# A Mamba mixer and cross-attention layer in fp32 on one core: the decay product in 64x64 tiles, its weights made by VectorE alone, keys loaded over 128 partitions

## What is computed

```python
h    = rmsnorm(x) * norm_w
gate, hid, B, C, dt = split(h @ in_proj.T)          # 8192, 8192, 8*128, 8*128, 128 wide
hid, B, C = silu(causal_conv(hid, B, C))            # 4 taps
dt   = softplus(dt + dt_bias);  A_cs = cumsum(-exp(A_log) * dt)
# 128 heads of 64, 8 groups of 16 heads; one chunk holds the whole sequence
M[i,j,h] = (C_i . B_j)[group of h] * exp(A_cs[i,h] - A_cs[j,h])   for j <= i, else 0
y[i,h]   = sum_j M[i,j,h] * hid[j,h] * dt[j,h] + Dp[h] * hid[i,h]
yg   = y * silu(gate);  yg = yg * rsqrt(mean over each group of yg**2) * gnorm_w
x    = layernorm(x + x + yg @ out_proj.T)
x    = layernorm(x + softmax(x @ ctx.T) @ ctx)       # per sequence
x    = layernorm(x + x @ W_base.T + b + 2 * (top-2 of 8 experts, rank 16))
```

## Time and profile before

| what | value |
|---|---|
| median of 3 runs | 1558.09 us (1551.89 to 1561.17) |
| profiled execution | 1558.3 us, span of its instructions 1556.6 us |
| busy share of the span | TensorE 95%, weight loads 77%, VectorE 69%, ScalarE 48%, GpSimd 43% |
| mean granted clock of TensorE | 0.978 of full |
| mixer, to about 1205 us of the span | TensorE all but always busy; transfers take 19 to 27% of the transfer engines |
| attention, from about 1250 us | transfer engines 98% busy at first, TensorE 79 to 85% |

### The profile page before, as it was taken

One profiled execution on the slowest core, in us unless ns is written; L12 is line 12 of the kernel. 1 busy time (PEld: TensorE's weight loads), 2 busy tenths in 40 slices (PEclk: granted clock), 3 DMA queues, 4 the chain that ended last, 5 costly groups with the idle time before them and its releaser, 6 DMA issues.

```text
span 1556.6 us, 25685 instructions
## 1 busy us (share of the span) xinstructions
PE 1471.4 (95%) x10492; PEld 1204.2 (77%) x10492; DVE 1071.3 (69%) x1248; ACT 754.2 (48%) x1003; POOL 661.6 (43%) x433
## 2 busy tenths in 40 slices
PE   5999999999999999999999999999999768889886
PEld 4888988898888889898989898989888534444442
DVE  5785878487757756774778477848784765767664
ACT  5764636462655355445546553646363254333330
POOL 6354537453645455454635554645373500001100
PEclk9999999999999999999999999999999879999998
DMA  4421212121312222121212121313120789888830
GB/s 149 122 80 57 87 51 92 55 83 49 92 52 69 62 79 68 52 82 58 82 38 93 55 83 48 93 45 88 50 82 7 181 187 211 191 183 206 188 72 12
DMA packets 53139, 141.52 MB, mean 91 GB/s; under 512 B 9684, under 2 KB 9812, under 8 KB 46858
## 3 DMA queue, kind: packets, MB, share of 16 engines
q1 hardware_dynamic: 51326, 136.20, 32.5%
q0 software_dynamic: 1696, 3.67, 1.0%
HBM read 135.72 MB, written 2.29 MB: 89 GB/s over the span
## 4 chain that ended last, share of the span: by engine, by line
PE 78%; issue 10%; DVE 6%; DMA 3%; ACT 2%; POOL 1%; SPq 0%; ACTq 0%; POOLq 0%; DVEq 0%
PE bank L1126 42%; PE bank L1193 20%; PE bank L1169 6%; PE bank L1156 3%; DMA x1p<-acc 2%; PE bank L1348 2%; PE bank L1321 1%; DVE conv L796 1%; DVE decay L849 1%; PE bank L1297 1%; DVE keysT L900 1%; PE bank L1180 0%; PE bank L1317 0%; DVE wo_lo L826 0%; DVE part L757 0%
## 5 line engine op out<-in xcount | busy, mean ns | idle before, releaser
L1126 PE MATMUL bank<-h_hi,w_hi 128*128 128x448 f32 x1152 | 337.5, 374 | 2.3 <-DVE conv L796 2.3
L1126 PE MATMUL bank<-h_lo,w_hi 128*128 128x448 f32 x1152 | 327.2, 365 | 0.0
L1126 PE MATMUL bank<-h_hi,w_lo 128*128 128x448 f32 x1152 | 326.6, 365 | 0.0
L796 DVE SCALAR_TENSOR_TENSOR conv<-bank,conv_w,conv 128x880 f32<-128x880 f32 (+2 forms) x240 | 268.1, 1117 | 79.4 <-ACT conv L571 73.7
L410 POOL TENSOR_TENSOR y_lo<-yg,y_hi 128x896 fp32r<-128x896 f32 x64 | 135.8, 2121 | 348.1 <-DVE mixw L859 202.2
L1126 PEld LDWEIGHTS bank<-h_hi,w_lo 128*128 128x128 f32 x1152 | 216.4, 188 | 17.3
L1126 PEld LDWEIGHTS bank<-h_lo,w_hi 128*128 128x128 f32 x1152 | 216.4, 188 | 17.0
L1126 PEld LDWEIGHTS bank<-h_hi,w_hi 128*128 128x128 f32 x1152 | 207.9, 188 | 24.2 <-DVE conv L796 3.2
L394 POOL TENSOR_TENSOR w_lo<-w_raw,w_hi 128x512 fp32r<-128x512 f32 x144 | 194.9, 1356 | 72.6 <-issue 36.4
L426 POOL TENSOR_TENSOR mixw<-decay,cbm 64x896 f32<-64x896 f32 x64 | 154.7, 2418 | 163.9 <-ACT decay L631 92.5
L837 DVE TENSOR_TENSOR hd_dt<-bank,dt_j 128x512 f32<-128x512 f32 x128 | 82.4, 686 | 177.7 <-PE bank L1156 177.5
(11 more groups left out here) (163 smaller groups left out, 2137.2 us busy)
## 6 DMA issues: line engine op xcount, KB each, us to landing
w_raw<-in_w_in SPq DMA_DIRECT2D x144, 256.0 KB, 2.9
decay<-cs_scratch SPq DMA_DIRECT2D x128, 196.0 KB
ring_a<-in_context SPq DMA_DIRECT2D x12, 1792.0 KB
ring_b<-in_context SPq DMA_DIRECT2D x12, 1792.0 KB
wo_raw<-in_w_out SPq DMA_DIRECT2D x64, 256.0 KB, 2.6
ring_a<-in_context SPq DMA_DIRECT2D x12, 208.0 KB
ring_b<-in_context SPq DMA_DIRECT2D x12, 208.0 KB
acc<-in_x SPq DMA_DIRECT2D x1, 1792.0 KB, 8.2
```

Source lines behind the costliest of these rows:

```text
L796: v.scalar_tensor_tensor(out=dst[:, :, sh:LEN], in0=src[:, :, 0:LEN - sh], scalar=conv_w[:, bass.ds(col, 1), TAPS - 1 - sh], in1=dst[:, :, ...
L1126: last = mm(place, w[:, k * P:(k + 1) * P], x[:, k, half * HALF:(half + 1) * HALF], start=(k == 0 and i == 0), stop=(k == KT - 1 and i == 2))
```

## The change

Four edits. First, `y_product` takes each sequence by itself: 64 rows by 64 channels stationary, 64 rows by 56 columns moving, so four small matmuls for a pair and not two: two row halves by two column halves of the array. The two sequences of a pair write to different banks of `yt` (even sequences bank 4, odd ones bank 5). `mixw` has no zero quarters and is half as wide, and every later buffer moves by that much. Second, VectorE makes the whole of `mixw` in one instruction over 128 partitions (`weigh`); GpSimd's `mix_low` and `after_mix_high`, and the zero fill, are gone, and one semaphore `m_done` stands for the two. Third, since even and odd sequences lie in two banks, `add_skip` is two instructions over 8 sequences each. Fourth, `load_unit` takes each sequence by itself, 128 partitions from a flat view of the rows (the last three rows belong to the next sequence and aren't used); the last sequence alone is cut in 112 and 13. VectorE also waits for its own `p_done` before the first `keys_part`.

```diff
-        mixw = sb("mixw", [P, 2, PAIRS, 2 * LEN], f32, mix)
+        mixw = sb("mixw", [P, 2, PAIRS, LEN], f32, mix)
...
+        def every_other(ap, b):
+            return ap.rearrange("p (q b) i -> p b q i", b=2)[:, b]
...
-            eng.wait_ge(unit_loaded[slot_of(unit)], 32 * (unit // RING + 1) + 16)
+            eng.wait_ge(unit_loaded[slot_of(unit)], 32 * (unit // RING + 1) + 16 * (unit // KR == PAIRS - 1))
...
# SP, load_cs
-                wait(sp, s["m_lo_done"], CT, g, c - 3)
-                wait(sp, s["m_hi_done"], CT, g, c - 3)
+                wait(sp, s["m_done"], CT, g, c - 3)
...
# SP, load_unit
-                src = A["context"][2 * u:2 * u + 2, :, r * UNIT:(r + 1) * UNIT]
-                for lo, hi in ((0, 112), (112, KP)):
-                    sp.dma_start(piece(unit)[lo:hi], src[:, lo:hi, :].rearrange("q p n -> p q n")
-                                 ).then_inc(unit_loaded[slot_of(unit)], 16)
-                if unit < RING:
-                    sp.dma_start(piece(unit)[KP:P], src[:, 0:P - KP, :].rearrange("q p n -> p q n")
-                                 ).then_inc(unit_loaded[slot_of(unit)], 16)
+                for q in range(2):
+                    first = (2 * (unit // KR) + q) * KP
+                    spans = ((0, P),) if first + P <= SEQS * KP else ((0, 112), (112, KP))
+                    for lo, hi in spans:
+                        sp.dma_start(piece(unit)[lo:hi, q, :],
+                                     rows[first + lo:first + hi, r * UNIT:(r + 1) * UNIT]
+                                     ).then_inc(unit_loaded[slot], 16)
...
# GpSimd
-            g_.memset(mixw[:].rearrange("p a b n -> p (a b n)"), 0.0)
...
-                    mix_low(g, st - 1)
-                    after_mix_high(g, st - 1)
...
# VectorE, add_skip
-                v.scalar_tensor_tensor(out=seqs(yg[:, c % 2, :]), in0=real(hid[:, c % 2, :]),
-                                       scalar=skip[:, bass.ds(g * CT + c, 1)], in1=bank_seqs(yt),
-                                       op0=ALU.mult, op1=ALU.add).then_inc(s["yres_done"], 1)
+                for b in range(2):
+                    last = v.scalar_tensor_tensor(out=every_other(seqs(yg[:, c % 2, :]), b),
+                                                  in0=every_other(real(hid[:, c % 2, :]), b),
+                                                  scalar=skip[:, bass.ds(g * CT + c, 1)],
+                                                  in1=yt[:, b, :].rearrange("p (q i) -> p q i", i=PAD)[:, :, 0:LEN],
+                                                  op0=ALU.mult, op1=ALU.add)
+                last.then_inc(s["yres_done"], 1)
...
# VectorE, mix_high becomes weigh
-                    out=mixw[PAD:P, :, :, LEN:2 * LEN],
-                    in0=decay[PAD:P, c % 4, :].rearrange("p (h q i) -> p h q i", h=2, i=LEN), scalar=1.0,
-                    in1=bc(cbm[PAD:P, :, :], 1, 2), op0=ALU.mult, op1=ALU.mult).then_inc(s["m_hi_done"], 1)
+                    out=mixw[:], in0=decay[:, c % 4, :].rearrange("p (h q i) -> p h q i", h=2, i=LEN), scalar=1.0,
+                    in1=bc(cbm[:], 1, 2), op0=ALU.mult, op1=ALU.mult).then_inc(s["m_done"], 1)
...
+                        dve.wait_ge(s["p_done"], GROUPS * CT)
                         keys_part(0, 0, 0)
...
# TensorE, y_product
-                    for h in range(2):
-                        place = yt[HD * h:HD * (h + 1), pair // 4, pair % 4 * P:(pair % 4 + 1) * P]
-                        last = mm(place.rearrange("p (s i) -> p s i", i=PAD)[:, :, 0:LEN],
-                                  hd_dt[:, pair, HD * h:HD * (h + 1)], mixw[:, h, pair, :], start=True, stop=True)
+                    for b in range(2):
+                        own_rows = slice(PAD * b, PAD * (b + 1))
+                        for h in range(2):
+                            last = mm(yt[HD * h:HD * (h + 1), b, pair * PAD:pair * PAD + LEN],
+                                      hd_dt[own_rows, pair, HD * h:HD * (h + 1)], mixw[own_rows, h, pair, :],
+                                      start=True, stop=True)
```

More of the change, by code:

```diff
@@ L181, in layer_kernel @@
             w_high w_low w_used tap0_done conv_tap silu_done gate_done t_done hd_done y_done yres_done
-            p_done y_high y_low sq_done sqsum_done d_done abs_done exp_done m_lo_done m_hi_done cb_done cbm_done
+            p_done y_high y_low sq_done sqsum_done d_done abs_done exp_done m_done cb_done cbm_done
             ss_done ss_picked ss_summed ms_done rg_done outa_done outa_evac outb_done psum_added sum_done
@@ L325, in _ @@
             over_groups(sp, group)
+            rows = A["context"].rearrange("s p n -> (s p) n")
             def load_unit(unit):
-                u, r = unit // KR, unit % KR
-                src = A["context"][2 * u:2 * u + 2, :, r * UNIT:(r + 1) * UNIT]
-                for lo, hi in ((0, 112), (112, KP)):
-                    sp.dma_start(piece(unit)[lo:hi], src[:, lo:hi, :].rearrange("q p n -> p q n")
-                                 ).then_inc(unit_loaded[slot_of(unit)], 16)
-                if unit < RING:
-                    sp.dma_start(piece(unit)[KP:P], src[:, 0:P - KP, :].rearrange("q p n -> p q n")
-                                 ).then_inc(unit_loaded[slot_of(unit)], 16)
+                r, slot = unit % KR, slot_of(unit)
+                for q in range(2):
[5 more added lines that the diff above has]
+                                     ).then_inc(unit_loaded[slot], 16)
             sp.wait_ge(s["w_used"], GROUPS * WT)
@@ L417, in add_squares @@
                 g_.tensor_tensor(out=sqsum[:], in0=sq[:], in1=sqsum[:], op=ALU.add).then_inc(s["sqsum_done"], 1)
[L419 to L434, removed]
-                wait(pool, s["m_hi_done"], CT, g, c + 1)
             def group_rms(g):
@@ L461, in _ @@
             pool.wait_ge(s["p_done"], GROUPS * CT)
-            pool.wait_ge(s["m_hi_done"], GROUPS * CT)
+            pool.wait_ge(s["m_done"], GROUPS * CT)
             pool.wait_ge(s["hd_done"], 2 * GROUPS * CT)
@@ L850, in differences, with weigh @@
                                 ALU.subtract).then_inc(s["d_done"], 1)
-            def mix_high(g, c):
+            def weigh(g, c):
                 if not within(g, c):
@@ L859, in mix_high @@
                 v.scalar_tensor_tensor(
-                    out=mixw[PAD:P, :, :, LEN:2 * LEN],
-                    in0=decay[PAD:P, c % 4, :].rearrange("p (h q i) -> p h q i", h=2, i=LEN), scalar=1.0,
-                    in1=bc(cbm[PAD:P, :, :], 1, 2), op0=ALU.mult, op1=ALU.mult).then_inc(s["m_hi_done"], 1)
+                    out=mixw[:], in0=decay[:, c % 4, :].rearrange("p (h q i) -> p h q i", h=2, i=LEN), scalar=1.0,
+                    in1=bc(cbm[:], 1, 2), op0=ALU.mult, op1=ALU.mult).then_inc(s["m_done"], 1)
             def mask_cb(g):
-                wait(dve, s["m_lo_done"], CT, g, 0)
-                wait(dve, s["m_hi_done"], CT, g, 0)
+                wait(dve, s["m_done"], CT, g, 0)
                 wait(dve, s["cb_done"], 1, g, 1)
@@ L926, in group @@
                         multiply_gate(g, st - 2)
-                    mix_high(g, st - 1)
+                    weigh(g, st - 1)
                     if not live:
@@ L1163, in y_product @@
                 wait(pe, s["hd_done"], 2 * CT, g, 2 * c + 2)
[L1164 to L1165 removed]
+                wait(pe, s["m_done"], CT, g, c + 1)
                 for pair in range(PAIRS):
[L1167 to L1170 removed]
+                    for b in range(2):
[4 more added lines that the diff above has]
+                                      start=True, stop=True)
                 last.then_inc(s["y_done"], 1)
```

4 lines of the change are left out of this document (1 added, 3 removed).

## The result

The changed kernel takes 1489.36 us (median of 4 runs, 1487.72 to 1492.33), the kernel before beside it 1557.95 us (4 runs, 1551.89 to 1561.17). The ratio is 0.957, with a 95% interval of 0.953 to 0.960: 4.3% faster. The forecast was 1518 us with a range of 1505 to 1542. The profiled execution took 1492.33 us, of which the span is 1490.6, against 1558.3 and 1556.6 before.

A forecast was written before the change was run, and what follows sets the result against it. The prediction took TensorE's own 12.47 us mixer step as the bound, a ScalarE and VectorE loop only 0.07 us shorter; 36.7 + 2.5 + 0.8 = 40.0 us off 1558.3 gave 1518 us, range 1505 to 1542.

The forecast's parts named there:

- The product: Decay product in the mixer: four tiles side by side, 16 turns, 1.08 us for 1.68; 36.7 us off in all.
- The bounds: For one decay product: 0.91 us if only columns counted, 2.02 us if only two tiles ran side by side.
- The floor of 25 ns: Rival for the decay product: about 25 ns for each matmul, so no change, 1555 to 1560 us; chance 0.07.
- all three terms: Decay product 36.7 us, first group 2.5 and the mixer's end 0.8, in sum 40.0 us off.
- VectorE and GpSimd: Mixer loop: `multiply_gate` 0.70 us shorter, `add_skip` 0.11 longer, loop 11.81 us against TensorE's step of 11.87; costed at nothing.
- The rival that the loop takes over: In the mixer, `weigh` takes 1.95 us, the loop 12.67; some 20 steps pay, 1534 us; chance 0.12.
- The first group: Mixer's first group, without output products to catch up in: some three `y_hi` intervals fall by 0.9, 2.5 us off.
- The loads of the keys: Attention: 2.4% more bytes in as many transfers; taken as nothing, 5 us either way.

The follow-up runs named there:

- undo_loads: The changed kernel with only the loads of the keys put back to 112 and 13 partitions, both sequences in each transfer; 1515.29 us.
- halves_back: The changed kernel with GpSimd making the lower half of the weights (partitions 0 to 63) again and VectorE the upper; 1510.7 us.
- loads_alone: The kernel before with nothing but the new `load_unit` and `wait_unit`; 1527.14 us, 0.981 of before.
- flat_112_16: The changed kernel with each sequence loaded as 112 and 16 partitions, a unit's rows following each other in DRAM without a gap; 1511.44 us.
- padded_cut_columns: The changed kernel with the context laid out with 128 rows per sequence, 128 partitions per transfer, each 8 KB row cut in two; 1482.14 us.
- both_128: The changed kernel with the context laid out with 128 rows per sequence, one 128-partition transfer carrying both sequences of a unit; 1484.41 us.
- cols_28: The changed kernel with the decay product on 28 of its 56 columns, half its output left unwritten; 1495.99 us.

## Why the prediction was wrong in size

**The product, right.** 1.08 us was forecast and 1.08 measured, behind a projection and behind `cb_product` alike, with 16 turns of four. The bounds are placed by the runs: fewer columns win almost nothing (1.06), two tiles side by side give 1.83 with 2.02 as the bound. Reading it off `cb_product` for the turn and off the score's first 0.11 us for the rate of issue was sound. The floor of 25 ns that the prediction weighs as a rival does not hold over all tiles: 64 matmuls in 1.08 us are 17 ns each. The term, 36.7 us, agrees with `undo_loads`, whose mixer is 38.9 us shorter than before against 40.0 for all three terms.

**VectorE and GpSimd, right in kind, and worth more than its price said.** `add_skip` in two costs 1.26 for 1.13, `multiply_gate` and `weigh` take 1.09 and 1.08. TensorE's idle before the projections stayed at 2.2 us. The rival that the loop takes over did not come. How much hung on it `halves_back` shows: with GpSimd's half in place three intervals in a row from `y_hi` to `y_hi` are 12.01, 13.76 and 12.54 us at the start of a group, for 11.45, 11.70 and 12.45 after, and 21 us of the gain are lost. The prediction had the mechanism, 0.70 us off `multiply_gate`, but it left out that GpSimd's half slowed two more instructions of the loop: the mean of `differences` fell from 1382 to 1086 ns and that of `wo_low` from 1013 to 858. And it had no price for the case without the relief.

**The first group, 2.1 us for 2.5, near enough.** In the profile of after, the output product of the first group starts 3.0 us earlier (119.09 to 116.09), and the four products ahead of it give 2.4, which seems to leave 0.6. But in that execution one projection ran long; first after, then `undo_loads`, which has the same mixer:

```profile
43.59 6.71 PE bank L1113 x24
```

```profile
43.62 5.14 PE bank L1111 x24
```

The granted clock from 43.5 to 51 us was 0.77 in the one and 1.00 in the other, and the kernel before has 5.14 us there too. In `undo_loads` the output product starts at 114.56, 4.5 us earlier than before, so 2.1 us came from the rounds that I let fall. The difference of 1.5 us is most of the 2.6 us by which the mixer's gain fell short in the profile of after; it belongs to that execution and not to the change.

**The loads of the keys, the failed step.** The prediction says: "If the rate per byte holds and loads bound the whole of a pair's 35 us, 2.4% is 0.8 us [...] I take nothing, and 5 us either way." The rate per byte did not hold: it went from about 240 to 420 GB/s. The attention fell by 28.6 us, and the table puts that down to the loads: they alone make 26.3 us of attention between `undo_loads` and after, and 31.4 between before and `loads_alone`. What I had looked at was the number of engines and of bytes, which hardly change. One reading could have warned me. The earlier trace rows show the transfers at seven to nine tenths in the attention, so that the waits there depend on their rate, and the term should have had a range for the rate and not for the bytes alone. With a faster rate the sum would have had the waits for `x1p` and the keys and the stalls in the scores on the side of the gain. How large the gain is, the trace of before does not tell. Its loads of weights over 128 partitions in the mixer (1084 to 1094 us, a quarter of a microsecond a figure) look fast at first:

```profile
GB/s 0 0 0 0 98 0 0 0 0 0 0 0 0 0 100 115 272 316 381 211 150 195 383 352 148 33 0 0 131 172 131 303 303 8 0 0 0 0 0 90
```

But at this resolution the old loads of the keys have such peaks too (1340 to 1350 us), so the peaks are no sign of the shape:

```profile
GB/s 197 180 213 262 148 148 98 246 229 213 393 295 426 213 279 311 246 262 360 262 442 262 131 279 164 311 66 295 131 197 197 66 98 131 66 131 33 131 33 0
```

A kernel with only the loads changed, as `loads_alone`, was needed to see it.

**Why 128 partitions.** The runs exclude more bytes or rows (112 and 16 load the same), an uneven deal over 16 engines (112, 16, 96, 32 and 64 all divide by 16, which is even by the rule that the prediction cites), DRAM's side (`flat_112_16`) and the number of transfers (`padded_cut_columns`). Of the causes that I could think of, what stays is which partitions one transfer writes at a time. The rates are medians over the microseconds of the attention in which such loads ran:

| cut | measured GB/s | estimate from the port map |
|---|---|---|
| 128 | 421 | 424 |
| 112 + 16 | 256 | 259 |
| 96 + 32 | 246 | 237 |
| 112 + 13 | 239 to 242 | 253 |
| 64 + 64 | 222 | 212 |
| 120 + 8 | 214 | 179 to 207 |

**How the rate became time.** Shown: the waits for `x1p` fell by 9.7 us, "issue" in the scores by 10.1, and both come back with the old loads. Argued: the copies of `x1p`, and whatever the scores' instructions need fetched, stand behind the keys in the same 16 engines, and free engines serve them sooner. The granted clock of the attention was 0.93 for 0.91 where TensorE stood idle 34.8 us for 53.8; that the one follows from the other is not shown.

## What to carry to other kernels

Load over all 128 partitions in one transfer, even if some rows are of no use: it moved keys at 420 GB/s for 240, and where rows of the next sequence or a padded layout fill the last partitions, it costs 2.4% more bytes; cut along the row if it must be cut. Before you price a change of a load at its bytes, ask what its new shape does to its rate, above all where transfers are busy beyond seven tenths; if the trace of before has no load of that shape under the same conditions, run a kernel with that load alone changed. When an engine's longest instruction goes, check what its neighbour's instructions take without it: the loop that was 0.07 us from being the bound is the one that decides whether the shorter product pays. And before you explain a microsecond or two between two profiles, compare the granted clock of the stretch where it arises.

The best version measured is the changed kernel with `padded_cut_columns`' or `both_128`'s loads, 1482 to 1484 us, which need the context laid out in DRAM with 128 rows for each sequence before the kernel starts.

## What the runs showed of the hardware

- A load of 128 partitions ran at 420 GB/s, the same rows as 112 and 16 at 256, 64 and 64 at 222, and 61 partitions at 25 to 27.
- Matmuls of 64x64 tiles, four side by side, started every 17 ns over a whole product (64 in 1.08 us); with two side by side a turn of two takes about 57 ns (63 in 1.83 us).
- VectorE's instruction of two SBUF inputs, 1.09 us alone, took 3.00 us where it ran beside GpSimd's of 2.57 for 2.05 us (`halves_back`).
- In `cols_28` the projection behind the product took 5.15 us for 5.06, with the same instructions. Its cause stays open.
- Idle time with no releaser in the profile ("issue", 13.7 us in the scores) went with faster transfers, to 3.6 us, without a change to the instructions there.
